# A local transformer kernel: the output product of a step moves ahead of the weighing of values on TensorE, and the residual sum ahead of the first division on VectorE

## The chip, the core and the metric

The kernel runs as one launch on one core of one Trainium2 chip. The metric is the device time of that launch in microseconds. The core has five engines, each with its own instruction stream in program order: TensorE (PE, matrix products into PSUM), VectorE (DVE), ScalarE (ACT), GpSimd (POOL) and SyncE (SP, which only issues DMAs here). They wait for each other through semaphores, which the kernel sets and awaits by hand.

## The reference

Inputs are two sequences of 1024 tokens with 128 features. Two adaptively normalised layers are computed; the change concerns the part of the first one that is a local transformer of six layers:

```python
def local_attention(q, k, v):        # windows of 32 queries, each sees 64 keys
    sim = jnp.einsum('bhwie,bhwje->bhwij', bq, bk2) * QK_SCALE
    sim = jnp.where(mask, -jnp.finfo(sim.dtype).max, sim)
    attn = jax.nn.softmax(sim, -1)
    out = jnp.einsum('bhwij,bhwje->bhwie', attn, bv2)
...
for i in range(DEPTH):               # DEPTH = 6, HEADS = 16, DIM_HEAD = 64
    x = attn_layer(shift_tokens(x), Wqkv[i], q_scale[i], k_scale[i], Wo[i]) + x
    x = ffn_layer(shift_tokens(x), ln_g[i], ln_b[i], W1[i], b1[i], W2[i], b2[i]) + x
```

`attn_layer` projects to queries, keys and values, normalises and rotates queries and keys, attends, and ends with `out @ Wo`. `ffn_layer` is layernorm, two products up (one goes through an exact gelu and multiplies the other) and one product down. Time mixing comes before these six layers; full attention over each sequence and eight experts come after.

## The kernel before

The local transformer is one software pipeline over 96 blocks (6 layers times 16 blocks of 128 tokens; `ALL` = 96, a block is `g`). Every engine runs the same loop `for i in STEPS` over steps -4 to 101, and in step `i` it handles different stages of several blocks. The order of the calls in the loop body of an engine is the order of its instructions; nothing is scheduled by a tool.

In step `i` TensorE does, in this order: the transposes of rotated queries and keys of block i (`turn_qk`, four, L624) interleaved with the query and key projections of block i+2 (`project_qk`, four, L607 to L609), the variance of a feed-forward (L717), the transposes of the attention output of block i-2 (`turn_att`, L692), the scores of block i (`scores`, L643 and L653, 128 small matmul records), the transposes of the probabilities of block i-1 (`turn_prob`, L664), two value projections of block i+1 (`project_v`), the weighing of the values by the probabilities of block i-1 (`weigh_v`, L682, again 128 small records), feed-forward parts, and the output product of block i-2 (`project_out`, L704).

The feed-forward works on pairs of blocks (`c`), so the loop has a period of two steps. In an odd step (`even(i, 5)` is a pair) TensorE has `up` (L726 and L727, three pairs of products), ScalarE has `gate` (L1068, three gelus, with a load of the gelu table before and a load of the exp and log table behind, L1070), and VectorE has `hidden` (L1359, three multiplications). In an even step TensorE has `down` (L735) and `center` (L712).

ScalarE empties most results out of PSUM. At the end of a step, after `gate` where there is one, it runs `invert_norms(i + 2)` (L999, L1001, L1003: relu, log, exp of the sums of squares), and then begins the next step with `empty_turned` (L1024, the transposed queries and keys) and `empty_qk` (L977). VectorE begins the next step with `normalise` (L1296), which waits for the last of `invert_norms`. In even steps ScalarE also runs `exponent(i - 1)` (L1041) after emptying everything of the first half, and `turn_prob(i - 1)` on TensorE waits for it.

VectorE runs in the second half of a step: `sum_squares` (L1289), `norm_att(i - 1, 0)` (L1337, the division of the weighed values by the sums of the probabilities, first half; it waits for `weigh_v`), `hidden` in odd steps, `add_residual(i - 2)` (L1343, waits for `project_out`), `norm_att(i - 1, 1)`.

Four PSUM banks (`TURN`) go round over all results that are emptied quickly. The dictionary `uses` lists their uses in the order of TensorE's program, and `wait_free` lets a use wait until the use four places ahead of it has been emptied:

```python
        def wait_free(eng, *use):
            n = uses[use] - len(TURN)
            ...
            kind, of, j = order[n]
            if kind == "turn":
                eng.wait_ge(S.turn_out, 4 * of + j + 1)
```

So the third transpose of queries and keys in a step waits until ScalarE has emptied the first one.

Of the kernel before, what the change touches and what calls it, by code (L numbers as in the profile page):

```python
# [74 lines left out]
def time_mixing_and_local(nc, A, sb, sem, bank, ident, mean_w, eps, x_main, h_in, h_mid, mod, gate_a):  # L75

    ALL = LAYERS * SLOTS
# [5 lines left out]
    with ExitStack() as ctx:  # L83
# [142 lines left out]
        def live(g):  # L226
            return 0 <= g < ALL

        def even(i, back):
            c = (i - back) // 2  # L230
            return c if (i - back) % 2 == 0 and 0 <= c < CHUNKS else None
# [34 lines left out]
        uses = {}  # L266
        for i in STEPS:
            for a in range(2):
                for j in (2 * a, 2 * a + 1):
                    if live(i):  # L270
                        uses["turn", i, j] = len(uses)
                for j in (2 * a, 2 * a + 1):
                    if live(i + 2):
                        uses["qk", i + 2, j] = len(uses)
            if live(i - 2):
                uses["att", i - 2, 0] = len(uses)
                uses["att", i - 2, 1] = len(uses)
            if i - 2 == ALL - 1:
                uses["out", i - 2, 0] = len(uses)
            if live(i - 1):  # L280
                uses["prob", i - 1, 0] = len(uses)
                uses["prob", i - 1, 1] = len(uses)
            if live(i + 1):
                uses["v", i + 1, 0] = len(uses)
            if even(i, 6) is not None:
                uses["down", even(i, 6), 0] = len(uses)
            if live(i + 1):
                uses["v", i + 1, 1] = len(uses)
            if even(i, 5) is not None:
                for j in range(FB):  # L290
                    uses["up", even(i, 5), j] = len(uses)
            if live(i - 2) and i - 2 < ALL - 1:
                uses["out", i - 2, 0] = len(uses)
        order = list(uses)

        def turn_bank(*use):
            return TURN[uses[use] % len(TURN)]
# [37 lines left out]
        with nc.Block(no_gpsimd_drain=True) as blk:  # L335
# [264 lines left out]
            def _(pe):  # L600
# [15 lines left out]
                def project_v(g, par):  # L616
                    project(g, ("v", g, par), WCH * (g // SLOTS) + 4 + par).then_inc(S.v_proj, 1)
# [78 lines left out]
                def project_out(g):  # L696
                    layer = g // SLOTS
                    if g % SLOTS == 0:
                        wait_layer(pe, layer)
                    wait_free(pe, "out", g, 0)  # L700
                    pe.wait_ge(S.att_out, 2 * (g + 1))
                    o = bank[:, turn_bank("out", g, 0), 0:BLK]
                    for hp in range(PAIRS):
                        mm = pe.matmul(o, w_o[:, layer % 2, hp, :], att_t[:, g % 2, hp, :], start=hp == 0,  # L704
                                       stop=hp == PAIRS - 1)
                    mm.then_inc(S.out, 1)
# [193 lines left out]
                for i in STEPS:  # L900
                    if i == -1:
                        group_mean(3)
                        project_output(2)
                        second_mean(2)
                        group_var(3)
                        second_var(2)
                    if i == 0:
                        project_output(3)
                        second_mean(3)
                    for a in range(2):  # L910
                        for j in (2 * a, 2 * a + 1):
                            if live(i):
                                turn_qk(i, j)
                        for j in (2 * a, 2 * a + 1):
                            if live(i + 2):
                                project_qk(i + 2, j)
                        if i == 0 and a == 0:
                            second_var(3)
                    if even(i, 5) is not None:
                        variance(even(i, 5))  # L920
                    if live(i - 2):
                        turn_att(i - 2, 0)
                        turn_att(i - 2, 1)
                    if i == ALL + 1:
                        project_out(ALL - 1)
                        last_mean(0)
                    if live(i):
                        scores(i)
                    if live(i - 1):
                        turn_prob(i - 1, 0)  # L930
                        turn_prob(i - 1, 1)
                    if live(i + 1):
                        project_v(i + 1, 0)
                    if i == ALL + 2:
                        center(CHUNKS - 1)
                    if even(i, 6) is not None:
                        down(even(i, 6))
                    if i == ALL + 2:
                        last_var(1)
                    if i == ALL + 3:  # L940
                        last_mean(2)
                    if i == ALL + 4:
                        last_mean(3)
                        last_var(3)
                    if i == ALL + 5:
                        last_mean(4)
                        last_var(4)
                    if live(i + 1):
                        project_v(i + 1, 1)
                    if live(i - 1):  # L950
                        weigh_v(i - 1)
                    if even(i, 4) is not None and i != ALL + 2:
                        center(even(i, 4))
                    if even(i, 5) is not None:
                        for j in range(FB):
                            up(even(i, 5), j)
                    if i == ALL + 1:
                        last_var(0)
                        last_mean(1)
                    if i == ALL + 3:  # L960
                        last_var(2)
                    if live(i - 2) and i - 2 < ALL - 1:
                        project_out(i - 2)

            @blk.scalar
            def _(act):
# [317 lines left out]
            def _(dve):  # L1284
# [255 lines left out]
                for i in STEPS:  # L1540
                    if i == -1:
                        add_logs(3)
                    if live(i + 1):
                        normalise(i + 1)
                    if i == -1:
                        second_scale(2)
                        group_norm(3)
                    if i == 0:
                        second_scale(3)
                        modulation(1)  # L1550
                    if live(i - 1) and even(i - 1, 5) is None:
                        sum_probs(i - 1)
                    if live(i):
                        shift_scores(i, 0)
                    if live(i - 1) and even(i - 1, 5) is not None:
                        sum_probs(i - 1)
                    if i == ALL + 1:
                        last_sum(0)
                        last_sum(1)
                    if even(i, 5) is not None:  # L1560
                        norm(even(i, 5))
                    if i == ALL + 1:
                        add_residual(ALL - 1)
                        last_sum(2)
                    if i == ALL + 2:
                        last_scale(0)
                    if i == ALL + 3:
                        last_scale(1)
                    if even(i, 6) is not None:
                        finish(even(i, 6))  # L1570
                    if i == ALL + 2:
                        last_sum(3)
                    if i == ALL + 4:
                        last_sum(4)
                        last_scale(3)
                    if i == ALL + 5:
                        last_scale(4)
                    if live(i):
                        shift_scores(i, 1)
                    if live(i + 2):  # L1580
                        sum_squares(i + 2)
                    if i == -1:
                        add_output(3)
                    if live(i - 1):
                        norm_att(i - 1, 0)
                    if even(i, 5) is not None:
                        for j in range(FB):
                            hidden(even(i, 5), j)
                    if i == ALL + 3:
                        last_scale(2)  # L1590
                    if live(i - 2) and i - 2 < ALL - 1:
                        add_residual(i - 2)
                    if live(i - 1):
                        norm_att(i - 1, 1)
                dve.wait_ge(S.ff_out, CHUNKS)
# [1078 lines left out]
```

## Time and profile before

| what | value |
|---|---|
| median of three runs | 2623.19 us (2614.48 to 2628.58) |
| profiled execution, its own time | 2625.65 us |
| its span, first to last instruction | 2623.9 us |
| TensorE busy | 2453.0 us, 93% |
| VectorE busy | 2159.1 us, 82% |
| ScalarE busy | 2037.2 us, 78% |
| GpSimd busy | 1518.5 us, 58% |

"Busy" is the time in which at least one instruction of the engine is executing. TensorE's matmuls are pipelined and overlap in the records, so one reads the distance from start to start for what a stage costs there. The granted clock of TensorE is a share of its full speed (1.00 is 2.4 GHz).

### The profile page before, as it was taken

The numbers are of one execution on the slowest core, as the hardware profiler recorded it, in microseconds if no ns is written. First come the engines' busy times: TensorE is split into PE (matmuls) and PEld (weight loads), VectorE is DVE, ScalarE is ACT, GpSimd is POOL, SyncE is SP. The second block draws the span as 40 slices with busy tenths as digits, with TensorE's granted clock in tenths as the row PEclk, the third lists the DMA queues.
The fourth block names the chain that finished last, engine by engine and source line by source line (L and its number), as shares of the span: only waits on it lengthen the run. The fifth ranks groups of instructions, "written<-read, shape, count | busy, mean of one in ns | idle before, by whom it ended". The sixth has DMA issues, their size and how long they took to land. (4 is left out here: it accounts for less than half of the span.)

```text
span 2623.9 us, 118567 instructions
## 1 busy us (share of the span) xinstructions
PE 2453.0 (93%) x52349; PEld 1966.4 (75%) x52349; DVE 2159.1 (82%) x2455; ACT 2037.2 (78%) x4077; POOL 1518.5 (58%) x1029
## 2 busy tenths in 40 slices
PE   6799999999999999999999999689999999997999
PEld 2488888888888888888888887467676776775787
DVE  5888888888888888888888887388888888885888
ACT  4688888889889888888888887566666666764676
POOL 3788887888788878888788785122222232322111
PEclk9899999999999999999999999899999999999999
DMA  3243433443334334333433333122222222221221
GB/s 96 56 94 92 106 77 92 92 106 83 93 93 113 80 89 102 96 83 93 97 94 79 85 85 71 36 54 52 60 61 58 50 61 60 57 53 34 82 73 41
DMA packets 275793, 202.01 MB, mean 77 GB/s; under 512 B 117568, under 2 KB 215880, under 8 KB 274248
## 3 DMA queue, kind: packets, MB, share of 16 engines
q1 hardware_dynamic: 275280, 194.42, 30.9%
q8 instruction: 414, 6.78, 1.1%
q14 instruction: 99, 0.81, 0.1%
HBM read 36.96 MB, written 1.11 MB: 15 GB/s over the span
## 5 line engine op out<-in xcount | busy, mean ns | idle before, releaser
L514 POOL TENSOR_TENSOR lt_t_sin<-lt_qk,lt_tab 128x512 f32<-128x512 f32 x384 | 682.8, 1799 | 243.9 <-DVE lt_qk L1296 241.8
L519 POOL TENSOR_TENSOR lt_qr<-lt_qr,lt_t_sin 128x1024 f32<-128x1024 f32 x192 | 457.8, 2385 | 28.2 <-POOL lt_t_sin L514 0.5
L2078 DVE TENSOR_REDUCE fa_neg_max<-bank 128x1 f32<-128x1024 f32 x256 | 301.6, 1220 | 94.7 <-PE bank L1875 93.3
L1901 PE MATMUL bank<-fa_prob_t,fa_v 32*64 32x128 f32 x16384 | 295.9, 277 | 18.9 <-issue 14.0
L2000 ACT ACTIVATE fa_prob<-bank,fa_neg_max 128x1024 f32<-128x1024 f32 x128 | 142.7, 1115 | 217.5 <-DVE fa_neg_max L2078 165.2
L1901 PEld LDWEIGHTS bank<-fa_prob_t,fa_v 32*64 32x64 f32 x16384 | 245.8, 131 | 81.3 <-issue 60.5
L2088 DVE STREAM_TRANSPOSE fa_prob_t<-fa_prob 128x1024 f32<-128x1024 f32 x256 | 302.1, 1219 | 0.0
L607 PE MATMUL bank<-lt_w_high,lt_x_high 128*128 128x512 f32 x576 | 262.8, 456 | 0.8 <-ACT lt_v_tok L1009 0.4
L1296 DVE TENSOR_TENSOR lt_qk<-lt_qk,lt_rn 128x2048 f32<-128x2048 f32 x96 | 236.3, 2461 | 5.9 <-ACT lt_rn L1003 2.2
L1289 DVE TENSOR_REDUCE lt_ssq<-lt_qr 128x32 f32<-128x2048 f32 x96 | 218.9, 2281 | 23.0 <-ACT lt_qr L985 23.0
L1303 DVE TENSOR_TENSOR lt_qr<-lt_qk,lt_tab 128x2048 f32<-128x2048 f32 x96 | 232.7, 2424 | 3.3
L977 ACT COPY lt_qk<-bank 128x512 f32<-128x512 f32 x384 | 220.4, 593 | 18.2 <-POOL lt_t_sin L514 2.8
L608 PE MATMUL bank<-lt_w_low,lt_x_high 128*128 128x512 f32 x576 | 228.4, 396 | 0.0
L609 PE MATMUL bank<-lt_w_high,lt_x_low 128*128 128x512 f32 x576 | 227.8, 396 | 0.0
L1316 DVE TENSOR_REDUCE lt_row_max<-bank 128x8 f32<-128x512 f32 x192 | 131.7, 686 | 113.4 <-PE bank L653 113.4
L624 PE MATMUL bank<-ident,lt_qr 128*128 128x128 f32 x1536 | 201.1, 274 | 14.7 <-POOL lt_qr L519 12.6
L985 ACT ACTIVATE lt_qr<-lt_qk 128x1024 f32<-128x1024 f32 x192 | 203.4, 1060 | 0.0
L624 PEld LDWEIGHTS bank<-ident,lt_qr 128*128 128x128 f32 x1536 | 177.5, 141 | 31.4 <-POOL lt_qr L519 15.7
L704 PEld LDWEIGHTS bank<-lt_prob_t,lt_w_o 128*128 128x128 f32 x1536 | 186.7, 192 | 8.1 <-issue 1.5
L704 PE MATMUL bank<-lt_prob_t,lt_w_o 128*128 128x128 f32 x1536 | 187.6, 275 | 1.0 <-ACT lt_prob_t L1035 0.8
L1807 POOL TENSOR_TENSOR fa_att_t<-fa_att,fa_inv_all 128x512 f32<-128x512 f32 x32 | 40.6, 1270 | 245.4 <-ACT fa_att L2024 245.4
L682 PEld LDWEIGHTS bank<-lt_v,lt_prob_t 64*32 64x32 f32 x12288 | 130.1, 105 | 66.7 <-issue 65.1
(260 smaller groups left out, 5912.5 us busy)
## 6 DMA issues: line engine op xcount, KB each, us to landing
lt_v<-lt_v_tok SPq DMA_DIRECT2D x576, 128.0 KB
fa_v<-fa_v_tok SPq DMA_DIRECT2D x256, 128.0 KB, 2.7
lt_v<-lt_v_tok SPq DMA_DIRECT2D x192, 64.0 KB
lt_k_t<-lt_k_t SPq DMA_DIRECT2D x84, 128.0 KB, 2.7
lt_v<-lt_v SPq DMA_DIRECT2D x168, 64.0 KB, 2.1
lt_w_raw<-in_lt_wqkv_dram SPq DMA_DIRECT2D x36, 256.0 KB
ex_cw_all<-cw_kept SPq DMA_DIRECT2D x8, 1024.0 KB, 4.5
lt_x_s<-h_in SPq DMA_DIRECT2D x96, 64.0 KB, 2.7
```

The costliest lines, as they stand in the source:

```text
L514: pool.tensor_tensor(dst[:, :, i, :], src[:, :, 1 - i, :], tab[:, g // 2 % 2, 1, at:at + 32].unsqueeze(1).to_broadcast([P, HEADS, 32]), AL ...
L519: pool.tensor_tensor(qr[:, g % 2, half], qr[:, g % 2, half], t_sin[:, :], ALU.add).then_inc(S.rotated, 1)
L607: pe.matmul(o, xh, w_high[:, k % WS, :], start=True, stop=False)
L608: pe.matmul(o, xh, w_low[:, k % WS, :], start=False, stop=False)
L609: return pe.matmul(o, xl, w_high[:, k % WS, :], start=False, stop=True)
L624: mm = pe.transpose(bank[:, turn_bank("turn", g, j), n * P:(n + 1) * P], qr[:, g % 2, (4 * j + n) * P:(4 * j + n + 1) * P], ident[:, :])
L704: mm = pe.matmul(o, w_o[:, layer % 2, hp, :], att_t[:, g % 2, hp, :], start=hp == 0, stop=hp == PAIRS - 1)
L1296: dve.tensor_tensor(heads, heads, r.unsqueeze(2).to_broadcast([P, 2 * HEADS, HD]), ALU.mult)\
L1303: dve.tensor_tensor(qr[:, g % 2, :].rearrange("p (a h d) -> p a h d", a=2, h=HEADS), qk[:, g % 2, :].rearrange("p (a h d) -> p a h d", a=2 ...
L1901: mm = pe.matmul(bank[d, 4 + a, 0:P].rearrange("p (u r) -> p u r", u=UPQ), v[rows, half % 2, kb, d], prob_t[rows, q % 2, par, :, 32 * kb:3 ...
L2078: dve.tensor_reduce(neg_max[:, u % 2, par:par + 1], bank[:, 2 * par:2 * par + 2, :].rearrange("p a n -> p (a n)"), AX.X, ALU.max, negate=T ...
L2088: dve.transpose(prob_t[:, q % 2, par, u % UPQ, :], prob[:, u % 2, par, :]).then_inc(S.turned, 1)
```

## The change

On TensorE, `project_out(i - 2)` moves from the end of the step to a place between the second value projection and `weigh_v(i - 1)`. Its place in the rotation of the four banks moves ahead of the three uses of `up` accordingly. On VectorE, `add_residual(i - 2)` moves from its place between the two divisions to a place ahead of the first one. No instruction is added or removed. The output product of the last block has a place of its own in both kernels and stays.

```diff
             if live(i + 1):
                 uses["v", i + 1, 1] = len(uses)
+            if live(i - 2) and i - 2 < ALL - 1:
+                uses["out", i - 2, 0] = len(uses)
             if even(i, 5) is not None:
                 for j in range(FB):
                     uses["up", even(i, 5), j] = len(uses)
-            if live(i - 2) and i - 2 < ALL - 1:
-                uses["out", i - 2, 0] = len(uses)
...
                     if live(i + 1):
                         project_v(i + 1, 1)
+                    if live(i - 2) and i - 2 < ALL - 1:
+                        project_out(i - 2)
                     if live(i - 1):
                         weigh_v(i - 1)
...
-                    if live(i - 2) and i - 2 < ALL - 1:
-                        project_out(i - 2)
...
+                    if live(i - 2) and i - 2 < ALL - 1:
+                        add_residual(i - 2)
                     if live(i - 1):
                         norm_att(i - 1, 0)
                     if even(i, 5) is not None:
...
                             hidden(even(i, 5), j)
                     if i == ALL + 3:
                         last_scale(2)
-                    if live(i - 2) and i - 2 < ALL - 1:
-                        add_residual(i - 2)
                     if live(i - 1):
                         norm_att(i - 1, 1)
```

TensorE in an odd step, from the last product of the value projections to the first transposes of the next step. Before:

```order
L609 MATMUL bank<-lt_w_high,lt_x_low 128x512
L682 MATMUL bank<-lt_v,lt_prob_t 32x64 x64
L726 MATMUL bank<-lt_f_norm,lt_w 128x256
L727 MATMUL bank<-lt_f_norm,lt_w 128x256
L726 MATMUL bank<-lt_f_norm,lt_w 128x256
L727 MATMUL bank<-lt_f_norm,lt_w 128x256
L726 MATMUL bank<-lt_f_norm,lt_w 85x256
L727 MATMUL bank<-lt_f_norm,lt_w 85x256
L704 MATMUL bank<-lt_prob_t,lt_w_o 128x128 x8
L624 MATMUL bank<-ident,lt_qr 128x128 x8
```

The same place in the changed kernel:

```order
L609 MATMUL bank<-lt_w_high,lt_x_low 128x512
L704 MATMUL bank<-lt_prob_t,lt_w_o 128x128 x8
L682 MATMUL bank<-lt_v,lt_prob_t 32x64 x64
L726 MATMUL bank<-lt_f_norm,lt_w 128x256
L727 MATMUL bank<-lt_f_norm,lt_w 128x256
L726 MATMUL bank<-lt_f_norm,lt_w 128x256
L727 MATMUL bank<-lt_f_norm,lt_w 128x256
L726 MATMUL bank<-lt_f_norm,lt_w 85x256
L727 MATMUL bank<-lt_f_norm,lt_w 85x256
L624 MATMUL bank<-ident,lt_qr 128x128 x8
```

The output product (L704) has moved ahead of the weighing and of all six products of `up`, which stand directly ahead of the next step's transposes now.

VectorE at the end of an odd step, from the sums of squares to the next step's first operation. Before:

```order
L1289 TENSOR_REDUCE lt_ssq<-lt_qr 128x32
L1337 TENSOR_TENSOR lt_prob<-bank,lt_row_sum 128x8x64
L1359 SCALAR_TENSOR_TENSOR lt_f_gate<-bank,lt_lvec,lt_f_gate 128x256 x2
L1359 SCALAR_TENSOR_TENSOR lt_f_gate<-bank,lt_lvec,lt_f_gate 85x256
L1343 TENSOR_TENSOR h_mid<-h_in,bank 128x128
L1337 TENSOR_TENSOR lt_prob<-bank,lt_row_sum 128x8x64
L1296 TENSOR_TENSOR lt_qk<-lt_qk,lt_rn 128x2048
```

The same place up to the first multiplications in the changed kernel:

```order
L1289 TENSOR_REDUCE lt_ssq<-lt_qr 128x32
L1343 TENSOR_TENSOR h_mid<-h_in,bank 128x128
L1337 TENSOR_TENSOR lt_prob<-bank,lt_row_sum 128x8x64
L1359 SCALAR_TENSOR_TENSOR lt_f_gate<-bank,lt_lvec,lt_f_gate 128x256 x2
```

The residual sum (L1343) now stands ahead of the first division and of the three multiplications.

## Rows read from the trace of the kernel before

**Rows 1.** The page: busy us, share of the span, instructions of each engine.

```profile
PE 2453.0 (93%) x52349; PEld 1966.4 (75%) x52349; DVE 2159.1 (82%) x2455; ACT 2037.2 (78%) x4077; POOL 1518.5 (58%) x1029
```

**Rows 2.** Stretches, start:end in us: two odd, an even, the whole loop.

```profile
core 0: us, PE busy (x) PEld busy (x) DVE busy (x) ACT busy (x) POOL busy (x), PEclk, DMA share, GB/s
592.58:608.76 16.18, 16.18 (x341) 13.86 (x340) 15.01 (x18) 15.27 (x29) 15.89 (x10) 1.00 0.40 98
608.76:623.46 14.70, 14.70 (x333) 12.67 (x332) 13.30 (x13) 12.69 (x26) 14.41 (x9) 1.00 0.27 58
943.61:961.74 18.13, 16.49 (x341) 14.01 (x340) 14.24 (x17) 15.36 (x28) 13.17 (x8) 1.00 0.40 94
110.59:1605.65 1495.06, 1440.25 (x31089) 1229.65 (x31090) 1266.52 (x1339) 1307.74 (x2430) 1225.21 (x690) 1.00 0.39 92
```

**Rows 3.** Timeline of TensorE, end of an odd step: start, duration, operation.

```profile
601.67 1.50 PE L682 MATMUL bank<-lt_v,lt_prob_t 64*32 64x64 f32 x128
603.11 0.70 PE L726 MATMUL bank<-lt_f_norm,lt_w 128*128 128x256 f32 x2
...
605.37 0.59 PE L727 MATMUL bank<-lt_f_norm,lt_w 128*85 128x256 f32 x2
605.80 1.95 PE L704 MATMUL bank<-lt_prob_t,lt_w_o 128*128 128x128 f32 x16
607.59 1.04 PE L624 MATMUL bank<-ident,lt_qr 128*128 128x128 f32 x8
...
609.86 1.03 PE L624 MATMUL bank<-ident,lt_qr 128*128 128x128 f32 x8
```

**Rows 4.** Timeline of ScalarE in the same stretch; idle time and releaser in brackets.

```profile
606.00 0.47 ACT L1068 ACTIVATE lt_f_gate<-bank,lt_lvec 85x256 f32<-85x256 f32 x1 [0.29 <-PE bank L727]
606.49 1.28 ACT L1070 ACT_TABLE_LOAD   x1
...
608.49 0.23 ACT L1003 ACTIVATE lt_rn<-lt_rn 128x32 f32<-128x32 f32 x1
608.63 1.06 ACT L1024 COPY lt_q_t<-bank 128x512 f32<-128x512 f32 x2
```

**Rows 5.** Timeline of VectorE in the same stretch.

```profile
605.32 0.68 DVE L1337 TENSOR_TENSOR lt_prob<-bank,lt_row_sum 128x512 f32<-128x512 f32 x1
605.91 1.25 DVE L1359 SCALAR_TENSOR_TENSOR lt_f_gate<-bank,lt_lvec,lt_f_gate 128x256 f32<-128x256 f32 x3
607.79 0.29 DVE L1343 TENSOR_TENSOR h_mid<-h_in,bank 128x128 f32<-128x128 f32 x1 [0.62 <-PE bank L704]
...
608.76 2.54 DVE L1296 TENSOR_TENSOR lt_qk<-lt_qk,lt_rn 128x2048 f32<-128x2048 f32 x1
```

**Rows 6.** Timeline of the even step behind it, ScalarE and TensorE.

```profile
611.64 1.29 ACT L977 COPY lt_qk<-bank 128x512 f32<-128x512 f32 x2
...
613.54 1.48 PE L653 MATMUL bank<-lt_k_t,lt_q_t 64*32 64x64 f32 x128
613.78 1.17 ACT L1041 ACTIVATE lt_prob<-lt_prob 128x512 f32<-128x512 f32 x2
...
615.00 1.09 PE L664 MATMUL bank<-ident,lt_prob 128*128 128x128 f32 x8
```

**Rows 7.** Timeline at the end of that even step, TensorE and VectorE.

```profile
618.72 1.48 PE L682 MATMUL bank<-lt_v,lt_prob_t 64*32 64x64 f32 x128
...
619.86 2.28 DVE L1289 TENSOR_REDUCE lt_ssq<-lt_qr 128x32 f32<-128x2048 f32 x1
...
622.05 0.68 DVE L1337 TENSOR_TENSOR lt_prob<-bank,lt_row_sum 128x512 f32<-128x512 f32 x1
```

**Rows 8.** Timeline of TensorE in a long odd step.

```profile
948.86 1.57 PE L653 MATMUL bank<-lt_k_t,lt_q_t 64*32 64x64 f32 x128
...
952.80 1.42 PE L682 MATMUL bank<-lt_v,lt_prob_t 64*32 64x64 f32 x120
955.85 0.32 PE L682 MATMUL bank<-lt_v,lt_prob_t 64*32 64x64 f32 x8 [1.64 <-issue]
```

**Rows 9.** Waits of TensorE in the loop: total us, times, longest.

```profile
PE bank L682 <- issue: 24.7, 25, 1.9
```

## The prediction

> **What bounds the kernel now.** I read the page first. TensorE shows most busy time, 93% of the span [rows 1]. Then I laid stretches of the loop side by side [rows 2]. A clean odd step (592.58 to 608.76) takes 16.18 us and a clean even step behind it 14.70 us, and in both TensorE is busy for the whole stretch at a granted clock of 1.00, while every other engine has idle time. So in clean steps TensorE's program is the bound, back to back. A clean pair takes 30.88 us. The whole loop took 1495.06 us for 93 steps, 32.15 us a pair, so 1.27 us of an average pair are pauses of some kind. One kind is seen in an odd step of 18.13 us, where TensorE was busy for 16.49 us only: it stopped for 1.64 us inside the weighing, 120 small products into it, waiting for nothing that the trace names [rows 8]. Such pauses in L682 sum to 24.7 us in 25 places [rows 9].
>
> The second thing to see is how little room lies behind the last product of `up`. In the clean odd step it ends at 605.96 [rows 3]. The last gelu starts at 606.00, after a wait for it, the table load runs from 606.49 to 607.77, the inverse norms end at 608.72, and ScalarE starts emptying the next step's transposes at 608.63 [rows 4]. VectorE's `normalise` starts at 608.76, 0.04 us behind the inverse norms [rows 5]. So the start of the next step on two engines hangs on the end of `up`. What covers this on TensorE is the output product that stands behind `up`: 1.79 us from its start to the next start (605.80 to 607.59) [rows 3].
>
> **The change, part by part.** Nothing is added. TensorE's total work is the same, and its first transposes of the next step stay at 607.59. What changes is when the pieces inside end.
>
> The output product earlier: its inputs were emptied in the first half of the step, so it adds no wait. Its consumer `add_residual` waited 0.62 us for it in this odd step [rows 5]. That wait goes, but it is worth nothing by itself, since `normalise` waits for ScalarE anyway. What is late next on VectorE is the last multiplication of `hidden`.
>
> `weigh_v` 1.79 us later: in the odd step it ends 601.67 + 1.50 + 1.79 = 604.96 [rows 3], and the first division started at 605.32 [rows 5]. With the residual sum (0.29 us, about 0.20 net of overlap) ahead, the division comes at about 605.5: no wait. In the even step it ends at 618.72 + 1.48 + 1.79 = 621.99, the sums of squares end at 622.14, and the division was at 622.05 [rows 7]. So even steps cost nothing. This is narrow: if the cover of about 0.1 us is missing, it costs a tenth of a microsecond a pair.
>
> `up` 1.79 us later, in odd steps: this is the term that costs. The last product ends at 607.75, the last gelu starts at 607.79, the inverse norms end at 610.51, `normalise` starts at 610.55, and ScalarE starts to empty transposes at 610.42 in place of 608.63 [rows 4, 5]. Two copies take 1.06 us [rows 4], so the first bank is free at 610.95. TensorE's third transpose, which needs that bank, stood at 609.86 [rows 3] with 0.70 us to spare (609.16 before). It now waits until about 611.0, 1.13 us. From there ScalarE leads. Before, it ran from 608.63 to the end of `exponent` at 614.95 [rows 4, 6], 6.32 us in one go, of which about 0.21 us was waiting (the two copies of L977 took 1.29 us [rows 6], where two copies take about 1.06 to 1.08 us [rows 4]). Without that wait it ends at 610.42 + 6.32 - 0.21 = 616.53, and `turn_prob` on TensorE starts at about 616.6 in place of 615.00. TensorE's scores ended at 615.02 [rows 6] and end at about 616.3 now, so ScalarE sets it. The pair loses 1.59 us. Later in the even step all engines keep their former distances, so nothing is given back.
>
> Bounds for this term: if only the bank wait counts, 1.13 us; if nothing is absorbed, 1.79 us. I take 1.59 us because the chain of rows gives it. The moved product stands in odd steps 5 to 95, 46 of them: 46 x 1.59 = 73 us, bounds 52 and 82.
>
> The pauses in the weighing: in the long odd step the scores start at 948.86 and the pause ends at 955.85, 6.99 us later [rows 8]. If that end is fixed by something that has been running since the scores, such as the delivery of instructions (the 128 products of scores or weighing start within 1.5 us, the densest stretches of TensorE's program), then 1.79 us of slow large products between them cover the pause of 1.64 us: the 120th product would come at about 956.0, after that end. In the clean even step 5.18 us lie between the starts of scores and weighing [rows 6, 7], in the long odd step 3.94 us [rows 8], and the even one has no pause. The bounds are nothing and 24.7 us [rows 9]. I take 85%, 21 us, since the case of rows 8 is covered just so. The rest of the 1.27 us a pair, some 33 us in the loop, lies elsewhere; I count none of it, and 12 us of it for the low end.
>
> The Trainium skill, in "Runtime: NRT & Kernel Launch", section "Instruction fetch mechanics", says that TensorE's instruction memory holds 2048 instructions, is refilled in blocks of 256, and that crossing a block is mostly hidden. Rows 8 and 9 speak against "hidden" if the pauses are fetches. By that rule they would be something else, and this term would be zero; that case is the first rival below.
>
> Sum against the profiled execution: 2625.65 + 73 - 21 = 2677.7 us. That execution was 2.5 us above the median of the three runs, so the median of the changed kernel should be about **2675 us**, 2% slower.
>
> **Rivals.**
> *The pauses stay* (they move with the instruction stream and strike in the weighing or in `up` all the same). For it: I know their place, not their cause. Against: the even step with more room has none. Then 2623 + 73 = 2696 us.
> *A smaller loss*: ScalarE regains more than 0.21 us in the even step, or TensorE's bank wait alone counts: 2623 + 52 - 21 = 2654 us. Against: ScalarE's chain in the even step is nearly without gaps.
> *Faster*: the late `up` is covered, because ScalarE's empties are not what TensorE waits for, and the covered pauses and the earlier residual sum remain. This needs 1.79 us of cover where the rows show 0.70 us at the third transpose; from that point on it decides. Price: -25 us, up to -37 with other pauses; 2595 us.
> *A balance*: the loss a pair is near 0.5 us and equals the 21 us of pauses; 2623 us.
>
> **How the numbers follow.** My forecast has a chance of 0.56 and a range of its own of 2664 to 2688. The pauses that stay have 0.16, the smaller loss 0.15, faster 0.08, a balance 0.05. The range from the bounds: low 2623 + 52 - 25 - 12 = 2638, high 2623 + 82 = 2705. It holds the first three cases. A measurement of this kernel can tell about 0.5%, 13 us, from no change. Slower by more than that: 0.56 + 0.16 + 0.15 = 0.87; within: 0.05; faster: 0.08.
>
> **What would show it.** In the trace of the changed kernel, odd steps (from one L1296 to the next) should be about 1.8 us longer in clean stretches, and even steps about 0.2 us shorter; L1296 behind an odd step should still start within 0.1 us of the end of L1003. TensorE should show new waits: L624 and L607 for ScalarE's L1024 and L977, about 1.1 us at the third transpose of even steps, and L664 for L1041 in every even step. VectorE's wait of L1343 for L704 should be gone, and L1359 should wait longer for the gelus. Pauses in L682 by "issue" should fall from 24.7 us to a few. The prediction is wrong if TensorE finds its banks free on time in even steps, if ScalarE's table load or gelus start earlier than the end of `up` implies, or if the pauses come back in another place.

## The result and the profile after

| | us |
|---|---|
| before, median of 4 runs beside the changed kernel | 2625.89 (2614.48 to 2633.98) |
| changed kernel, median of 4 runs | 2673.42 (2665.38 to 2675.94) |
| ratio, 95% interval | 1.0179 [1.0134, 1.0224] |
| predicted | 2675 (2638 to 2705) |

The change makes the kernel 1.8% slower. The profiled execution took 2675.94 us, with a span of 2674.2 us.

First the stretches of the changed kernel: a clean odd step, the even step behind it, and the loop from the third to the last of the 96 L1296 (93 steps), which are the same ends as in [rows 2].

```profile
core 0: us, PE busy (x) PEld busy (x) DVE busy (x) ACT busy (x) POOL busy (x), PEclk, DMA share, GB/s
940.02:958.13 18.11, 17.60 (x346) 14.80 (x344) 14.14 (x17) 15.40 (x28) 13.20 (x8) 1.00 0.51 123
958.13:972.50 14.37, 13.60 (x327) 11.95 (x328) 12.63 (x14) 12.48 (x26) 11.63 (x6) 1.00 0.30 72
109.59:1652.54 1542.95, 1450.04 (x31094) 1238.85 (x31094) 1276.05 (x1339) 1301.10 (x2430) 1227.69 (x690) 1.00 0.38 89
```

Against [rows 2], the odd step went from 16.18 to 18.11 us and the even one from 14.70 to 14.37 us, so this clean pair costs 32.48 in place of 30.88 us, 1.60 us more, measured on VectorE. Measured on TensorE, from first transpose (L624) to first transpose two steps later, it is 32.34 in place of 30.88 us, 1.46 us more; the odd step has its old 16.0 us and the whole loss lies in the even one (14.86 to 16.33 us). The loop went from 1495.06 to 1542.95 us, 47.9 us more; that is nearly all of the difference of the two spans, 50.3 us. TensorE is no longer busy all the time in clean steps. The granted clock stayed at 1.00 in these stretches.

Now the end of that odd step in order of time, all engines; it answers to [rows 3], [rows 4] and [rows 5].

```profile
949.20 1.95 PE L704 MATMUL bank<-lt_prob_t,lt_w_o 128*128 128x128 f32 x16
951.07 1.48 PE L682 MATMUL bank<-lt_v,lt_prob_t 64*32 64x64 f32 x128
...
952.92 0.28 DVE L1343 TENSOR_TENSOR h_mid<-h_in,bank 128x128 f32<-128x128 f32 x1
...
953.12 0.68 DVE L1337 TENSOR_TENSOR lt_prob<-bank,lt_row_sum 128x512 f32<-128x512 f32 x1
...
954.75 0.59 PE L727 MATMUL bank<-lt_f_norm,lt_w 128*85 128x256 f32 x2
...
955.18 1.04 PE L624 MATMUL bank<-ident,lt_qr 128*128 128x128 f32 x8
955.38 0.47 ACT L1068 ACTIVATE lt_f_gate<-bank,lt_lvec 85x256 f32<-85x256 f32 x1 [0.39 <-PE bank L727]
955.87 1.28 ACT L1070 ACT_TABLE_LOAD   x1
955.89 0.48 DVE L1359 SCALAR_TENSOR_TENSOR lt_f_gate<-bank,lt_lvec,lt_f_gate 85x256 f32<-85x256 f32 x1 [0.38 <-ACT lt_f_gate L1068]
...
957.87 0.23 ACT L1003 ACTIVATE lt_rn<-lt_rn 128x32 f32<-128x32 f32 x1
958.01 1.05 ACT L1024 COPY lt_q_t<-bank 128x512 f32<-128x512 f32 x2
958.13 2.29 DVE L1296 TENSOR_TENSOR lt_qk<-lt_qk,lt_rn 128x2048 f32<-128x2048 f32 x1 [1.17 <-ACT lt_rn L1003]
958.72 1.06 PE L624 MATMUL bank<-ident,lt_qr 128*128 128x128 f32 x8 [1.10 <-ACT lt_q_t L1024]
...
964.06 1.09 PE L664 MATMUL bank<-ident,lt_prob 128*128 128x128 f32 x8 [0.19 <-ACT lt_prob L1041]
```

Read it from the last `up` product (954.75, ending at 955.34): nothing of TensorE stands between it and the next step's transposes at 955.18. The gelu, the table load and the inverse norms follow it as before, and now they end 2.9 us after the first transposes have started, where it was 1.1 us [rows 3, 4]. VectorE waits 1.17 us for the inverse norms, and TensorE waits 1.10 us at the third transpose for ScalarE to empty the first one. From first transpose to `turn_prob` (L664) the rows of before give 615.00 - 607.59 = 7.41 us [rows 3, 6], and these give 964.06 - 955.18 = 8.88 us: 1.47 us more.

The sums over the whole execution, from the view of waits of the changed kernel (engine and line, who was waited for: total us, times, longest):

```profile
ACT lt_f_gate L1068 <- PE bank L727: 97.4, 138, 2.6
...
DVE lt_qk L1296 <- ACT lt_rn L1003: 54.7, 47, 1.2
PE bank L624 <- ACT lt_q_t L1024: 52.9, 45, 2.1
...
PE bank L664 <- ACT lt_prob L1041: 16.1, 31, 1.8
...
PE bank L653 <- issue: 8.8, 11, 2.2
...
PE bank L682 <- issue: 5.0, 9, 1.1
...
DVE h_mid L1343 <- PE bank L704: 3.5, 3, 2.0
```

TensorE has a new wait of 52.9 us in 45 places, about once a pair; before it was 2.1 us in one place. The pauses in the weighing fell from 24.7 us in 25 places [rows 9] to 5.0 us in 9, and those in the scores (L653) rose from 4.7 to 8.8 us. VectorE's wait for the output product is down from 41.7 to 3.5 us, and that is worth nothing, as its wait for the inverse norms shows.

### The profile page after: what moved, and what is told of

Read it like the earlier page. It is cut to its first block and busy times, and to the rows that moved or that the text cites. A ratio compares the mean times of both kernels' runs of the same rounds, so it can differ in the third digit from the quotient of the medians.

```text
span 2674.2 us, 118567 instructions
## 1 busy us (share of the span) xinstructions
PE 2463.9 (92%) x52349; PEld 1976.7 (74%) x52349; DVE 2168.5 (81%) x2455; ACT 2029.8 (76%) x4077; POOL 1522.4 (57%) x1029
## 5 line engine op out<-in xcount | busy, mean ns | idle before, releaser
L1296 DVE TENSOR_TENSOR lt_qk<-lt_qk,lt_rn 128x2048 f32<-128x2048 f32 x96 | 240.3, 2504 | 54.9 <-ACT lt_rn L1003 54.7
L624 PE MATMUL bank<-ident,lt_qr 128*128 128x128 f32 x1536 | 203.4, 276 | 68.2 <-ACT lt_q_t L1024 52.9
L607 PE MATMUL bank<-lt_w_high,lt_x_high 128*128 128x512 f32 x576 | 263.4, 457 | 1.6 <-issue 0.8
L624 PEld LDWEIGHTS bank<-ident,lt_qr 128*128 128x128 f32 x1536 | 177.6, 142 | 107.8 <-issue 71.8
L977 ACT COPY lt_qk<-bank 128x512 f32<-128x512 f32 x384 | 218.6, 608 | 15.4 <-PE bank L609 4.4
L704 PEld LDWEIGHTS bank<-lt_prob_t,lt_w_o 128*128 128x128 f32 x1536 | 187.1, 192 | 9.5 <-issue 1.0
L704 PE MATMUL bank<-lt_prob_t,lt_w_o 128*128 128x128 f32 x1536 | 187.8, 275 | 0.8 <-ACT lt_prob_t L1035 0.8
L2006 ACT ACTIVATE fa_prob<-bank,fa_neg_max 128x512 f32<-128x512 f32 x256 | 173.3, 682 | 0.0
```

Source lines behind the costliest of these rows:

```text
L607: pe.matmul(o, xh, w_high[:, k % WS, :], start=True, stop=False)
L624: mm = pe.transpose(bank[:, turn_bank("turn", g, j), n * P:(n + 1) * P], qr[:, g % 2, (4 * j + n) * P:(4 * j + n + 1) * P], ident[:, :])
L1296: dve.tensor_tensor(heads, heads, r.unsqueeze(2).to_broadcast([P, 2 * HEADS, HD]), ALU.mult)\
```

## The experiments

**Which steps carry the loss.** The move is made in one parity of steps alone; the same condition stands at the bank's use, at the call on TensorE and at the residual sum on VectorE (for even steps `is` and `is not` change places).

```diff
-                    if live(i - 2) and i - 2 < ALL - 1:
+                    if even(i, 5) is not None and live(i - 2) and i - 2 < ALL - 1:
                         project_out(i - 2)
...
+                    if even(i, 5) is None and live(i - 2) and i - 2 < ALL - 1:
+                        project_out(i - 2)
```

> The move is made in the steps with the feed-forward's up products alone (odd steps); even steps keep the old order. My theory, that the last product of up, then ScalarE's gelu, table load and inverse norms set the next step: the whole loss stays and the pauses in the weighing of odd steps still go, 2665 to 2685 us, ratio about 1.018. Rival, that the later weighing costs in every step (each division 1.8 us later): about half of the loss, 2645 to 2652 us.

> The move is made in even steps alone; odd steps keep the old order. My theory: no cost and no gain, since the pauses are in odd steps and even steps had cover for the division: 2615 to 2632 us, ratio 0.997 to 1.003. Rival, that the later weighing costs in every step: 2645 to 2652 us.

Odd steps alone: 2675.16 us, ratio to before 1.0167 [1.0121, 1.0214]. Even steps alone: 2636.16 us, 1.0026 [1.0005, 1.0047], within the expected ratio and 4 us above the expected time. The loss comes from the move in odd steps, as the chain over `up` says; a cost of the later weighing in every step, of the size that the rival named, is excluded. But the pauses did not behave as I expected. With the move in odd steps alone, TensorE's pauses by "issue" were these (its lines are numbered a little higher; L684 is the weighing, L655 the scores, L626 the transposes):

```profile
PE bank L626 <- ACT lt_q_t L1028: 53.2, 45, 2.3
...
PE bank L684 <- issue: 13.6, 15, 2.1
PE bank L655 <- issue: 12.7, 15, 2.0
```

Step by step, with pauses over 0.1 us counted, the weighing of odd steps kept 8.1 of its 21.9 us (3.9 with the full change), the scores of even steps rose from 3.5 to 10.0 us and the weighing of even steps from 3.0 to 5.6 us: 26.3 us for both lines by the view of waits, where the full change has 13.8 us. In the run with even steps alone they sum to 27.2 us in the weighing and 8.2 us in the scores, against 24.7 and 4.7 us before, 6.0 us more, about what that run lost (0.0026 of 2629 us is 7 us).

**The table load.** Both kernels with a relu in place of the gelu and without the load of the other table behind it. Their output is another one: the feed-forward has a relu. With the gelu the load ahead of it goes too: the traces have 4 table loads in place of 100. That one was not on the path: in the odd step of the changed kernel shown above it ran from 951.18 to 952.46, and the first gelu then waited for `up` until 953.66.

```diff
-                        act.activation(f_gate[0:m, j, :], bank[0:m, turn_bank("up", c, j), 0:PAIR], ACT.Gelu,
+                        act.activation(f_gate[0:m, j, :], bank[0:m, turn_bank("up", c, j), 0:PAIR], ACT.Relu,
                                        bias=lvec[0:m, layer % 2, 6 + j:7 + j]).then_inc(S.gated, 1)
-                    act.preload_act_table_set("natural_log_exp_and_others")
```

> The changed kernel with a relu in place of the gelu of the feed-forward and without the preload behind it, so its output is another and ScalarE loads no tables in the loop; the rest is unchanged. My theory: ScalarE's chain behind up is 1.28 us shorter, which is more than the 1.1 us that TensorE waits at the third transpose, so the loss goes nearly whole: 2585 to 2610 us. Rival, that VectorE's late multiplications and division make the loss: they depend on up, not on the table load, so 2660 to 2675 us.

> The kernel before with the same relu and without the preload (its output is another). The control of the run above: TensorE is the bound there in clean steps, so the 1.28 us bring only the 0.6 us that the transposes of probabilities wait for ScalarE in half of the even steps: 2605 to 2618 us. If ScalarE were the bound before too, it would fall by 46 x 1.28 = 59 us, to 2564 us.

The changed kernel took 2601.79 us, 0.9892 [0.9849, 0.9935] of before; the kernel before with the same edit took 2618.25 us, 0.996 [0.9939, 0.998]. The edit gives the kernel before some 11 us and the changed kernel some 72 us. This is the plainest evidence for the chain: shorten it by 1.28 us behind `up` and the loss is gone. In the changed kernel with the relu, L624 waits for ScalarE for 1.0 us in all in place of 52.9 us, and the pauses stay about as they were (its three leading rows in the loop, that of the weighing and that of this wait):

```profile
PE bank L664 <- ACT lt_prob L1041: 13.4, 24, 1.8
PE bank L653 <- issue: 10.1, 10, 2.0
PE bank L624 <- POOL lt_qr L519: 8.8, 4, 3.5
...
PE bank L682 <- issue: 4.6, 9, 1.3
...
PE bank L624 <- ACT lt_q_t L1024: 1.0, 5, 0.2
```

With the relu on both sides the very same move makes the kernel faster, by 16.5 us. The kernel before with the relu had pauses of 25.5 us in the weighing and 3.8 us in the scores, 29.3 us, and this one has 14.7 us. The 14.6 us between them are nearly the gain. The reason that I had given for the control was not right, though its time was at the edge of the range: `turn_prob` (L664) waits for ScalarE as long as before, 13.5 us and not less than 13.7. In the loop of the two traces the relu is worth 5 us there; where the 11 us of the medians come from is open.

**The two halves of the change.** TensorE's part alone leaves the residual sum behind the multiplications, VectorE's part alone leaves the output product at the end of the step:

```diff
+                    if live(i - 2) and i - 2 < ALL - 1:
+                        add_residual(i - 2)
                     if live(i - 1):
                         norm_att(i - 1, 0)
```

> TensorE's part of the change alone: the output product moves, the residual sum stays between multiplications and second division on VectorE. My theory: the chain over up is the same, so 2665 to 2690 us; in odd steps the first transpose of the next step now waits for the bank of the output product until the residual sum behind the three multiplications, about 0.9 us, which is less than the wait for ScalarE that follows, so it adds 0 to 15 us at most. Rival, that the early residual sum causes the loss: 2600 to 2625 us.

> VectorE's part alone: the residual sum stands ahead of the first division, the output product stays at the end of the step on TensorE. The residual sum then waits for the output product with the division and the three multiplications behind it, and these start about 2 us late in odd steps; they free the banks of the next step's first transposes. My theory: slower, 46 x 1.5 to 2 us plus some in even steps (the second division about 0.7 us later than the output product's end), 2690 to 2730 us, by VectorE and the banks and not by ScalarE. Rival: VectorE has enough idle time to take it, 2620 to 2640 us.

TensorE's part alone took 2671.94 us, 1.0196 [1.0167, 1.0226] of before, so the whole loss comes from that half. The wait changed its name, since the first transposes now wait for the bank that the late residual sum frees, and what ScalarE would have cost at the third transpose is hidden in it (I had expected 0.9 us for the first and a longer wait for the second; the first is 1.36 us each time and the second is left once):

```profile
PE bank L624 <- DVE h_mid L1343: 59.9, 44, 1.4
```

VectorE's part alone took 2696.93 us, 1.0299 [1.0266, 1.0331]. This is one odd step of it:

```profile
620.27 1.95 PE L704 MATMUL bank<-lt_prob_t,lt_w_o 128*128 128x128 f32 x16
622.25 0.29 DVE L1343 TENSOR_TENSOR h_mid<-h_in,bank 128x128 f32<-128x128 f32 x1 [2.11 <-PE bank L704]
...
622.96 0.23 ACT L1003 ACTIVATE lt_rn<-lt_rn 128x32 f32<-128x32 f32 x1
623.06 1.25 DVE L1359 SCALAR_TENSOR_TENSOR lt_f_gate<-bank,lt_lvec,lt_f_gate 128x256 f32<-128x256 f32 x3
623.68 1.06 PE L624 MATMUL bank<-ident,lt_qr 128*128 128x128 f32 x8 [1.46 <-DVE lt_f_gate L1359]
```

The residual sum waits 2.11 us with everything of VectorE queued behind it, and the multiplications free the bank that the first transposes need. ScalarE is on time here. So the two halves belong together: the residual sum may stand ahead only because the output product does.

**Other orders.** If the late end of `up` is what costs, the small products of the weighing can be what stands last. In odd steps they go behind `up`, once from the kernel before and once from the changed one; on VectorE the multiplications come ahead of the first division.

```diff
-                    if live(i - 1):
+                    if live(i - 1) and even(i, 5) is None:
                         weigh_v(i - 1)
...
                             up(even(i, 5), j)
+                    if live(i - 1) and even(i, 5) is not None:
+                        weigh_v(i - 1)
```

> The kernel before with the weighing moved behind up in odd steps and on VectorE the three multiplications ahead of the first division and the residual sum last. up ends 1.0 to 1.4 us earlier, and 2.7 us of large products stand between scores and weighing. My theory: TensorE stays the bound, nothing is late, and the pauses of the weighing (24.7 us) go: 2595 to 2612 us, ratio 0.990 to 0.996. Rival, that the pauses follow the dense stretch wherever it stands: 2615 to 2630 us.

> The changed kernel with the weighing behind up in odd steps (output product, up, weighing) and the three multiplications ahead of the first division. up now ends 0.3 us later than before the change and not 1.8 us, within the 0.7 us of cover. My theory: the loss of the change goes and the pauses stay away: 2598 to 2620 us. Rival, that the late weighing (it ends last in the step, at about the start of the next) makes VectorE's divisions late: they would end about 0.1 to 0.5 us later than before, up to 2640 us.

From the kernel before (`up`, weighing, output product; residual sum last): 2620.38 us, 0.9993 [0.9978, 1.0008], no difference. The pauses in the weighing fell to 6.4 us, but my claim that nothing is late was wrong: `up` now comes so early that it waits for its input, the shifted norm from ScalarE.

```profile
PE bank L726 <- ACT lt_f_norm L1060: 22.3, 47, 1.5
```

47 waits of 22.3 us in all eat the 18 us.

From the changed kernel (output product, `up`, weighing): 2591.29 us, 0.9885 [0.9857, 0.9913], faster than both kernels by a clear margin, and 7 us faster than the best that I had expected. One odd step of it:

```profile
591.33 1.95 PE L704 MATMUL bank<-lt_prob_t,lt_w_o 128*128 128x128 f32 x16
...
593.12 0.60 PE L726 MATMUL bank<-lt_f_norm,lt_w 128*128 128x256 f32 x2
...
595.28 0.59 PE L727 MATMUL bank<-lt_f_norm,lt_w 128*85 128x256 f32 x2
...
595.80 1.48 PE L682 MATMUL bank<-lt_v,lt_prob_t 64*32 64x64 f32 x128
...
598.40 0.23 ACT L1005 ACTIVATE lt_rn<-lt_rn 128x32 f32<-128x32 f32 x1
598.67 2.78 DVE L1298 TENSOR_TENSOR lt_qk<-lt_qk,lt_rn 128x2048 f32<-128x2048 f32 x1
```

The output product fills the time in which `up` would wait for its input (that wait is 1.2 us in one place here), and the weighing stands behind `up` as a cover for ScalarE's chain. Pauses in the weighing are down to 1.4 us in 4 places, but those in the scores are 9.5 us, twice what they were before; both together are 10.9 in place of 29.4 us. These 18.5 us are most of the gain of 30 us; another 3.5 us is `turn_prob`'s shorter wait for ScalarE, and the rest is not traced. The price is that VectorE waits 27.8 us in 53 places for the weighing; of this TensorE feels 1.4 us, in one place (L692).

**Where the pauses go, and what they are.** The last two kernels are the one above with even steps in their old order, and the kernel before with half of the weighing's products done twice.

```diff
-                    for hp in range(PAIRS):
+                    for hp in (*range(PAIRS), *range(PAIRS // 2, PAIRS)):
```

> The order output product, up, weighing in odd steps alone; even steps as before the change. Even steps alone gained nothing from the move (ratio 1.0026), so if each step counts for itself this equals the version with the move in all steps: ratio 0.987 to 0.991, 2588 to 2600 us. Rival, seen in the run with the move in odd steps alone, where the pauses in the weighing of even steps rose from 2.3 to 6.3 us and in their scores from 3.5 to 10.6 us: the pauses have to be kept out of both, and this version is 8 to 15 us slower than that one, ratio 0.991 to 0.995.

> The kernel before, with the second half of the weighing's products done twice (the same result), so 192 in place of 128 dense records with as many weight loads. The work itself costs 95 x 0.74 = 70 us where TensorE is the bound. If the pauses come from the delivery of instructions, a longer dense stretch exhausts what is at hand more often: pauses in the weighing rise from 24.7 us to 80 us or more, and the kernel takes 2740 us or more. If they are events in time that fall on the weighing by chance, they rise by the longer stretch at most, to about 37 us, and it takes 2700 to 2710 us.

With even steps in their old order: 2605.34 us, 0.9938 [0.9918, 0.9959], as the rival said. The pauses come back in the weighing (11.0 us in 14 places, against 1.4 us), nearly all of them in even steps, while those in the scores are 7.5 us against 9.5, so the two sums differ by 7.6 us. The two loops, from the third to the last `normalise`, differ by 6.4 us (1474.96 and 1468.52 us), which the pauses account for. The medians differ by 14 us; the rest is not explained by the loop.

The longer dense stretch took 2810.81 us, 1.0715 [1.069, 1.074]. Its row of the waits, and one of its pauses with what stands behind it:

```profile
PE bank L682 <- issue: 112.8, 72, 2.3
...
636.83 0.63 PE L653 MATMUL bank<-lt_k_t,lt_q_t 64*32 64x64 f32 x36 [1.81 <-issue]
637.38 1.94 PE L664 MATMUL bank<-ident,lt_prob 128*128 128x128 f32 x8
```

Half as many products more made the pauses 4.6 times as long in total, 72 places in place of 25. Events that fall on the stretch by chance would have given 37 us. Of the 187 us, the work itself is 60 us (192 products take 2.11 us, 0.63 us more a step), the pauses in the weighing are 88 us, and other pauses of TensorE with no named releaser, in the scores and elsewhere, some 13 us. The rest, some 26 us, is about what the clock can have taken: behind the pause above the granted clock is 0.50, the lower level of 1.2 GHz, and eight transposes took 1.94 us where they take 1.09 us [rows 6]. The mean granted clock of the run is 0.974, and 0.984 in the kernel before; by an estimate from these two, (1 - 0.974) x 2810 less (1 - 0.984) x 2624, that is up to 31 us. In the changed kernel the granted clock of the loop is 1.00, as before.

**What a pause waits for.** The page of the profile lists a DMA queue that carries instructions, with the same 414 packets in the kernel before, in the changed one and in every other kernel here; only the kernel with the longer stretch has more (queue: packets, MB, share). First the kernel before, then that one:

```profile
q8 instruction: 414, 6.78, 1.1%
...
q8 instruction: 462, 7.57, 1.2%
```

The longer stretch adds 96 x 64 products, each with a weight load, 12,288 instructions, and 48 packets: one packet (16,384 bytes) for 256 instructions of TensorE. Count TensorE's instructions in a trace (weight loads, products, semaphore operations, drains and the one branch), and all 386 pauses over 0.1 us inside scores and weighing, in all twelve traces, end at count 194 or 195 above a multiple of 256, and between 1.0 and 1.6 us (median 1.4 us) after such a packet has landed. The pause of [rows 8] ended at 955.85; its packet was under way from 953.26 to 954.53. So a pause is the wait for the next block of 256 instructions.

Most crossings from one block to the next cost nothing. What decides is the time since the last crossing. In the kernel before, of 188 crossings inside scores and weighing, 16 of 18 paused when it was less than 3 us, 9 of 46 at 3 to 4 us, 5 of 17 at 4 to 5 us, 2 of 35 at 5 to 6 us and none of 72 beyond 6 us. The next packet starts about 1.0 us after a crossing (median), takes about 1.0 us, and the engine goes on 1.4 us after it has landed, so some 3.4 us a block is what the delivery allows; 256 instructions of the weighing are used up in 1.48 us.

## Why the prediction was right

**The bound and the cover.** It named TensorE's back-to-back program as the bound, and too little cover at the third transpose for the 1.79 us by which `up` moves; both hold. It predicted that ScalarE starts to empty the transposes 2.83 us after the first of them has started, and the trace has 2.83 us (955.18 to 958.01). It said that the third transpose would stand 1.13 us later. The profile marks 1.10 us as idle, but from first to third transpose the time went from 2.27 to 3.54 us, 1.27 us more. The cover was 0.52 us and not 0.70: the first copy takes 0.57 us and not half of 1.06, and TensorE starts 0.14 us behind its end. The prediction said that `normalise` would start within 0.1 us of the end of the inverse norms; it starts at 958.13, 0.03 us behind (957.87 + 0.23). The relu run of the changed kernel confirms the link through ScalarE.

**The size of the loss.** Predicted were 1.59 us a pair. From first transpose to next step's first transpose, TensorE's even steps grew from 15.30 to 16.83 us (mean of 45), 1.53 us, of which 0.04 us are pauses, and 1.47 us in the clean step shown. The path to that number is not quite the predicted one. The third transpose takes 1.27 us of it. The prediction let ScalarE recover 0.21 us on its way to the end of `exponent`; in the clean step it recovered 0.33 us (5.99 us from 958.01, in place of 6.32). It said that L664 would wait for L1041 in every even step, as a wait that wasn't there before. The wait (over 0.05 us) is there in 37 of 45 even steps, but it had been there in 36, and over the whole loop its sum rose from 13.7 to 16.1 us only, because TensorE's own delay takes up most of ScalarE's. The forecast wait of L607 for L977 does not show either. (TensorE's scores would by its own terms have ended at 616.15 and not at "about 616.3"; the sum does not use this.) That nothing is given back later in the even step holds: from L664 to the next first transpose it is 7.61 us before and 7.58 us after.

**The pauses.** Predicted was 21 us back from the weighing; measured were 24.7 - 5.0 = 19.7 us, of which 8.8 - 4.7 = 4.1 us came back in the scores. The prediction had named pauses that come back in another place as a sign of being wrong; they did, in part. So net 15.6 us. Odd steps as a whole shrank from 16.89 to 16.43 us, 0.46 us, of which 0.40 us are pauses. Over 46 pairs that is 70 us lost and 21 us gained, 49 us, against 73, 21 and 52 us in the forecast, 47.9 us in the loop and 47.5 us in the medians. That the total is this close owes a little to luck: the third transpose cost more than its term, `turn_prob` less.

**Even steps.** "Cost nothing" was nearly right: the move there alone cost 0.26%, with 6.0 us more of pauses, and not by the division, whose wait for the weighing was 7.0 us in the whole changed kernel and 2.8 us before.

**The skill's rule.** The Trainium skill ("Runtime: NRT & Kernel Launch", "Instruction fetch mechanics") calls the crossing of instruction blocks mostly hidden. Its blocks of 256 instructions are what these traces show. "Mostly hidden" is right for the count: in the kernel before, 32 of 188 crossings inside scores and weighing paused. It is not for the cost, where stretches are dense: the pauses of the weighing were 0.9% of the time before, and 112.8 us, 4%, with the denser stretch. The prediction's first rival drew from that rule that the pauses are something else; they are fetches, as its own term had supposed.

## What to carry to other kernels

When an engine's program is full, moving a block within it is not free: whatever is passed ends later by the length of the block, and what hangs on its end counts. Before moving a stage, follow the longest chain that leaves the stages it passes (here `up`, gelu, table load, inverse norms, first empty of the next step) and compare its length with what the engine still has to do before it needs the result. The stage with the longest chain behind it goes first, the one whose result is needed latest goes last, and waits that vanish from an engine off that path, such as the residual sum's, are no gain.

If an engine pauses with no named releaser, look at the DMA queue of its instructions before calling the pause noise.

## What the runs showed that I had not expected

Pauses of TensorE with no named releaser are waits for blocks of 256 instructions, and they strike where two crossings follow each other within less than some 3 to 5 us. In the clean steps of the kernel before, 3.8 us lie between the starts of scores and weighing in odd steps and 5.2 us in even ones, and odd steps have 21.9 of the 24.9 us of pauses over 0.1 us in the weighing. But this distance alone does not tell: with the output product moved in odd steps alone it is 6.1 us there (median), and 8.1 us of pauses are left; what else decides when a block comes late is open. The large products moved between two dense stretches took 19.7 us of pauses away from the weighing, 15.6 us net, without a change in the work.

The same edit to ScalarE's chain (relu for gelu, no table loads) is worth 11 us where TensorE's program covers the chain and 72 us where it doesn't, in kernels that differ by the place of one product and one sum.
